# A fused two-layer transformer kernel on one core: where the second attention's negated maxima are copied, and the order of its score products

## What is computed

```python
q = _apply_rotary((x @ wq).reshape(b, s, H, HD), cos, sin)
k = _apply_rotary((x @ wk).reshape(b, s, H, HD), cos, sin)
v = (x @ wv).reshape(b, s, H, HD)
scores = jnp.einsum('bqhd,bkhd->bhqk', q, k) * scale
scores = jnp.where(causal[None, None], scores, jnp.finfo(scores.dtype).min)
probs = jax.nn.softmax(scores, axis=-1)
out = jnp.einsum('bhqk,bkhd->bqhd', probs, v).reshape(b, s, d)
return out @ wo
```

## Time and profile before

| | us |
|---|---|
| median of 3 runs (lowest, highest) | 2004.17 (2003.63, 2010.52) |
| the profiled execution, its own time | 2012.39 |
| its span | 2010.7 |
| first and last copy of maxima (L2018) start at | 1598.4, 1856.3 |
| busy in the span: PE, DVE, ACT, POOL | 1913.5, 1515.4, 914.2, 905.4 |
| mean granted TensorE clock, as a share of full speed | 0.982 |

### The profile page before, as it was taken

The page is one execution under the profiler, slowest core; times in us unless marked ns, Lnnn a source line. Parts: engine busy times, 40 slices in busy tenths (PEclk is TensorE's granted clock), DMA queues, the critical chain, the costliest instruction groups (busy, mean ns, idle before and its releaser), DMA issues.

```text
span 2010.7 us, 41714 instructions
## 1 busy us (share of the span) xinstructions
PE 1913.5 (95%) x14040; PEld 1626.3 (81%) x14040; DVE 1515.4 (75%) x2386; ACT 914.2 (45%) x2297; POOL 905.4 (45%) x872
## 2 busy tenths in 40 slices
PE   8999979999999999999999999988999889998998
PEld 3688869999999999999999999976898755555776
DVE  2576657787777887777888777877888457778886
ACT  1323334444444444444444444445455357777432
POOL 0123354444444444444444444453576557777111
PEclk9999989999999999999999999998999989999999
DMA  9567751111111111111111111411487764443121
GB/s 344 173 209 239 229 161 47 47 47 47 47 47 47 47 44 43 45 43 44 47 47 47 47 47 42 140 35 48 146 252 216 229 193 146 146 142 117 38 63 58
DMA packets 201695, 211.02 MB, mean 105 GB/s; under 512 B 19066, under 2 KB 172666, under 8 KB 200604
## 3 DMA queue, kind: packets, MB, share of 16 engines
q1 hardware_dynamic: 200692, 209.27, 33.6%
q10 hardware_dynamic: 936, 0.85, 0.1%
HBM read 128.14 MB, written 73.53 MB: 100 GB/s over the span
## 4 chain that ended last, share of the span: by engine, by line
PE 68%; issue 13%; DVE 9%; POOL 3%; ACT 3%; SPq 2%; DMA 1%; POOLq 0%; ACTq 0%; DVEq 0%
PE ps L1029 18%; PE ps L990 18%; PE ps L1004 7%; PE ps L1018 4%; PE ps L1041 4%; DVE f_neg_max L1977 3%; PE ps L1013 3%; PE ps L2587 2%; POOL k_rot L565 2%; PE ps L2551 2%; ACT f_q L2018 2%; PE ps L1798 2%; PE ps L2086 2%; PE ps L2092 1%; SPq L1305 1%
## 5 line engine op out<-in xcount | busy, mean ns | idle before, releaser
L1029 PE MATMUL ps<-wo,ot 128*128 (+1 forms) x1536 | 391.0, 404 | 0.1
L1029 PEld LDWEIGHTS ps<-wo,ot 128*128 128x128 f32 x1536 | 283.7, 191 | 61.1 <-issue 1.3
L990 PE MATMUL ps<-ht_hi,wq 128*128 (+1 forms) x2048 | 288.2, 284 | 3.9 <-DVE q_swap L863 3.9
L990 PEld LDWEIGHTS ps<-ht_hi,wq 128*128 128x128 f32 x2048 | 269.0, 192 | 9.7 <-DVE q_swap L863 4.1
L790 ACT ACTIVATE prob<-ps,neg_max 128x128 f32<-128x128 f32 (+1 forms) x512 | 208.3, 421 | 130.1 <-DVE neg_max L870 108.0
L947 POOL TENSOR_TENSOR q_rot<-q_rot,q_swap 128x512 f32<-128x512 f32 x128 | 164.9, 1288 | 201.5 <-DVE q_swap L863 196.9
L797 ACT ACTIVATE pt<-ps 128x512 fp32r<-128x512 f32 x192 | 107.7, 597 | 302.8 <-PE ps L1041 302.8
L942 POOL TENSOR_TENSOR prob<-prob,inv_sum 128x512 f32<-128x512 f32 x64 | 66.6, 1040 | 291.0 <-DVE inv_sum L879 291.0
L1977 DVE TENSOR_REDUCE f_neg_max<-ps 128x4 f32<-128x512 f32 (+1 forms) x128 | 122.3, 957 | 62.4 <-PE ps L2086 60.6
L990 PE MATMUL ps<-ht_lo,wq 128*128 (+1 forms) x1024 | 165.5, 284 | 0.0
L1004 PE MATMUL ps<-pt,vv 128*128 128x512 f32 x576 | 148.7, 402 | 9.3 <-issue 8.6
(11 more groups left out here) (245 smaller groups left out, 4168.5 us busy)
## 6 DMA issues: line engine op xcount, KB each, us to landing
stack_dram<-e_part SPq DMA_DIRECT2D x192, 128.0 KB, 2.4
v_dram<-v_part SPq DMA_DIRECT2D x32, 512.0 KB, 5.7
k_dram<-k_part SPq DMA_DIRECT2D x64, 256.0 KB, 2.7
kk<-k_dram SPq DMA_DIRECT2D x128, 128.0 KB, 2.1
vv<-v_dram SPq DMA_DIRECT2D x128, 128.0 KB, 2.1
f_q<-stack_dram SPq DMA_DIRECT2D x124, 104.0 KB
f_k<-stack_dram SPq DMA_DIRECT2D x124, 104.0 KB
wmod<-in_wmod SPq DMA_DIRECT2D x12, 1024.0 KB, 11.8
```

Source lines behind the costliest of these rows:

```text
L990: mm = nc.tensor.matmul(ps_q[j][:, e], w[:, c:c + HD0], r[:, bass.ds(u % B, 1), k].rearrange("p o s -> p (o s)"), start=(n == 0), stop=(n ...
L1029: mm = nc.tensor.matmul(ps_y[j][:], o[:, j, h * P:(h + 1) * P], w[:, bass.ds(at + h * D, D)], start=(n == 0), stop=(n == len(passes) - 1))
```

## The change

The second copy of the negated maxima no longer reads PSUM: it is issued behind the unit's two exponentials in ScalarE's step, and reads the first copy from SBUF. The late scores wait for the first copy alone. `near` is computed ahead of `far` and of the early scores, and both wait for both exponentials of the unit before; the exponentials and the cuts follow in the order near, far. The exponential that waits for VectorE's first maximum is now the second of the two.

```diff
--- before.py
+++ after.py
@@ -2014,8 +2014,12 @@
 
             act.wait_ge(m_done, u + 1)
             src = max_rows.rearrange("p (o s) -> p o s", o=1).broadcast_to([HU, 2, S])
-            for e in range(2):
-                nc.scalar.activation(q[slot][64 * e:64 * e + HU], src, ACT.Identity).then_inc(m_out, 1)
+            nc.scalar.activation(q[slot][0:HU], src, ACT.Identity).then_inc(m_out, 1)
+
+        def negated_again(u, slot):
+
+            act.wait_ge(m_out, 2 * u + 1)
+            nc.scalar.activation(q[slot][64:64 + HU], f32(q[slot][0:HU]), ACT.Identity).then_inc(m_out, 1)
 
         def high(w):
 
@@ -2026,9 +2030,9 @@
         def exponentials(u, slot, at):
             if at >= 2:
                 act.wait_ge(o_done, u - 1)
-            for j, (p, sc) in enumerate(((prob1, t1), (prob0, t0))):
+            for j, (p, sc) in enumerate(((prob0, t0), (prob1, t1))):
                 act.wait_ge(t_done, 4 * u + 2 * j + 2)
-                if j == 0 and at < U - 2:
+                if j and at < U - 2:
                     act.wait_ge(smax, 2 * u + 5)
                 nc.scalar.activation(p[slot % 2][:].rearrange("p (e i) s -> p e i s", e=2), sc, ACT.Exp,
                                      scale=SCALE1).then_inc(p_exp, 1)
@@ -2038,6 +2042,8 @@
                 negated(v + 1, (slot + 1) % NS)
             if 0 <= at < U:
                 exponentials(v, slot, at)
+            if -1 <= at < U - 1:
+                negated_again(v + 1, (slot + 1) % NS)
             if at in (0, 1):
                 load_unit(act, keep, NS + v, v)
             if 5 <= at and slot % 2:
@@ -2052,7 +2058,7 @@
     def gpsimd(pool):
         def cut(u, slot):
 
-            for j, p in enumerate((prob1[slot % 2][:], prob0[slot % 2][:, :, 0:P])):
+            for j, p in enumerate((prob0[slot % 2][:, :, 0:P], prob1[slot % 2][:])):
                 pool.wait_ge(p_exp, 2 * u + j + 1)
                 nc.gpsimd.nop(nofuse=True)
                 nc.gpsimd.affine_select(p, p, pattern=[[0, HU], [1, P]], compare_op=ALU.is_ge, fill=0.0,
@@ -2095,7 +2101,7 @@
     def scores_late(pe, u, slot, first=False):
 
         if not first:
-            pe.wait_ge(m_out, 2 * u)
+            pe.wait_ge(m_out, 2 * u - 1)
         for e in range(2):
             put_mask(1, e)
         for e in range(2):
@@ -2181,20 +2187,17 @@
             if 0 <= at < U:
                 pe.wait_ge(m_out, 2 * v + 2)
                 if at > 0:
-                    pe.wait_ge(p_exp, 2 * v - 1)
+                    pe.wait_ge(p_exp, 2 * v)
                 if at < U - 2:
                     mask_early()
+                shifted_near(v, slot)
                 shifted_far(v, slot)
             if 0 <= at < U - 2:
                 scores_early(pe, v + 2, (slot + 2) % NS)
-            if 0 <= at < U:
-                if at > 0:
-                    pe.wait_ge(p_exp, 2 * v)
-                shifted_near(v, slot)
             if -1 <= at < U - 2:
                 scores_late(pe, v + 2, (slot + 2) % NS)
             if at == U - 1:
-                pe.wait_ge(p_exp, 2 * U - 1)
+                pe.wait_ge(p_exp, 2 * U)
             if at >= TAIL:
                 side(pe, at - TAIL)
             if 1 <= at:
```

## The result

The change takes 1992.28 us (median of 6 runs, 1989.61 to 1992.67), the kernel before, in runs beside it, 2006.26 (6 runs, 2003.63 to 2010.52). The ratio is 0.9926, 95% interval 0.9913 to 0.9939: 14.8 us less. The forecast was 1990.2 us, 14.0 less than a kernel before of 2004.2. The profiled execution of the change took 1990.09 us, its span is 1988.4.

What follows compares the result with a forecast made beforehand. No engine is full; a loop of waits through TensorE, ScalarE and VectorE sets the 3.84 us step. Middle 11.7 + opening 2.2 + tail 1.0 - end 0.9 = 14.0 us less, from 2004.2 to 1990.2 us; range 1985 to 1999.

Steps and rivals of the forecast that it cites:

- The loop: Middle step of the second attention: the chain of waits from transposes to next transposes falls from 3.84 to 3.58 us.
- TensorE is late next: Middle step: of 0.60 us taken off the loop only 0.26 are gained, as TensorE's own work delays the late mask.
- the middle: The 45 middle steps of the second attention: 0.26 us gained in each, 11.7 us in all; 5.9 with the upper bound.
- granted clock below 1.00 in the middle steps: A sign in the profile of the change that would show the forecast wrong: TensorE below full clock there.
- The other paths: Four paths in a middle step, among them VectorE's reductions and ScalarE's second copy, that must fit into 3.58 us.
- The rivals: Middle, late second copy: wait only moves (step 3.84 at 1.10 us of copy), chance 0.09; slower (from 1.4 us), 0.06.
- The opening: First steps of the second attention, with two waits for loads: 2.2 us gained, bounds 1 and 3.
- The tail: Six steps with pieces of the next stage: 4.05 us each instead of 4.22, 1.0 us gained; bounds 0.5 lost, 2.5 gained.
- The end: Last unit: the next stage's product waits for both exponentials instead of the small one alone, 0.9 us lost.

Runs made afterwards that it cites:

- the edit of the last unit: The change, but in the last unit alone far, its exponential and its cut come first and the next stage's product waits for that exponential only: 1990.47 us, ratio 0.9913.

## Why the prediction was right, and where it was not

**The loop.** The prediction's sum for a step was 3.58 us, measured is 3.54, or 3.53 without the first step. The mechanism is as predicted, and shown from both sides: without the copy's move the late mask stays at 1.66 and the step at 3.84, and the masks' wait for ScalarE, 8.6 us before, is gone in the change. "TensorE is late next" is shown too: taking the early mask out of TensorE's way gave 3.36. The term that was mis-sized is the way from the transposes to the late mask, 1.36 instead of 1.40, and with it the middle, 13.7 instead of 11.7. That TensorE's blocks keep their sum when they are permuted held within 0.04 us here; with `far` behind the late scores it did not hold. The sign "granted clock below 1.00 in the middle steps" came true in the first of the 45 steps alone, as it had before the change.

**The other paths.** VectorE's first reduction was put at 1.57 to 1.68 after the transposes with "up to 0.07" lost; it starts at 1741.94 - 1740.44 = 1.50, and nothing is lost. The late reduction still waits for TensorE, but by 0.07 us a step only. The second copy was put at 0.63 us from a copy of 128 partitions; it takes 0.627. The Trainium skill's page "ScalarE: Activation LUTs" (section What ACT_TABLE_LOAD costs) had given an estimated 0.61; the trace's 0.627 lies 2 to 3% above it.

**The price of a late copy.** The rivals said that the step returns to 3.84 with a copy of 1.10 us. The loop is there, but its constant is 2.5 to 2.6 us, not 2.74, and the point is near 1.35. In the step shown with 1.32 us of copies the chain is the prediction's, and its links tell where the 0.26 went: early mask to first reduction 1.29 (1746.28 to 1747.57) where the sum had 1.36; the exponential of `far` ends at 1748.89, but the first copy starts at 1748.79, 0.10 before, where the sum put it behind; and the three copies take 1.24 from the first start to the last end where they add up to 1.32. So the overlap of one ScalarE instruction with the next was left out, though the prediction had read 0.1 of it in the pair of exponentials. The rivals with this loop had a chance of 0.15 between them; the run with the old order of exponentials shows such a loop deciding, at 4.03 a step.

**The opening.** Predicted 2.2; the two executions of the change give 3.5 and 2.3. From the first transposes to the load that TensorE waits for it is 38.74 us (40.13 before), 1.4 less for the 1.1 predicted, and from there to the next transposes 4.18 (4.71), 0.53 for 0.6. The rest lies behind that load: the next three steps, of which the prediction counted 0.24, take 10.70 us (11.88 before), with 3.63 at a granted clock of 0.97 in the first of them (4.20 at 0.83 before). The two executions of the change differ in the wait for that load (5.35 and 4.29), in the wait for the next one (0.95 and 1.64), and in the fourth step, 4.50 us at 0.76 in one and 5.96 at 0.51 in the other. The size stays open: over all kernels here the opening takes 56.8 to 64.9 us, and which steps run at the lower clock was not tried.

**The tail.** Predicted 4.05 a step, measured 3.94, and the reason given was for the most part wrong. ScalarE was said to hold it, with its first copy late. A step of the change:

```profile
1827.59 1.28 POOL L2070 TENSOR_TENSOR f_both<-f_prob,f_prob 128x512 f32<-128x512 f32 x1
...
1827.96 0.57 ACT L2017 ACTIVATE f_q<-ps 4x512 fp32r<-4x512 f32 x1
...
1828.30 1.12 DVE L2443 TENSOR_TENSOR g_lo<-g_raw,g_w 128x512 fp32r<-128x512 f32 x1
...
1828.61 0.39 PE L2098 MATMUL ps<-mask_b,ident_b 128*128 128x256 bf16 x2
...
1829.34 1.81 DVE L1977 TENSOR_REDUCE f_neg_max<-ps 128x4 f32<-128x512 f32 x2
...
1831.21 0.38 PE L2129 MATMUL ps<-ident,f_neg_max 128*4 128x128 f32 x2 [0.55 <-DVE f_neg_max L1977]
```

The copy ends at 1828.53, ahead of the late mask at 1828.61; in two of the six steps the mask does wait for it, 0.22 us. VectorE holds: g_lo (L2443) ends at 1829.42 and both reductions follow it with no idle time, and the transposes wait for them (0.55). Over the six steps VectorE is busy for 23.42 of 23.63 us, before for 23.25 of 25.34, when it waited for the late scores. The overlap of f_both with g_lo, which the prediction weighed with the Trainium skill's page "GPSIMD Engine Reference" (section Specifications), did not go away: f_both runs from 1827.59 to 1828.87, over g_lo's start. The eight g_lo of the change take 0.97 to 1.14 us, where before 1.35 and 0.69 took turns. That agrees with the page's contention of two-input instructions, and the 2.0 us that would have come back by it did not. It is not overlap as such that makes g_lo long, as the prediction read the earlier trace rows: the short g_lo before (1835.19 to 1835.88) overlaps an f_both too, but one that starts behind it, at 1835.42, and then f_both is the long one, 1.59 us for 1.27. Where f_both started first, g_lo ended 0.54 to 0.55 us behind its end, before (1831.80 and 1832.34) and in the change (1828.87 and 1829.42). In the change f_both starts first in all of the six steps. What came back, 1.7, is the idle time of VectorE, and the order alone brings it, as the run without the copy's move shows (23.67); which part of the order does it was not tried.

**The end.** Predicted 0.9 lost; 0.94 in the profile, and 0.98 given back by the edit of the last unit. The span's end is a further 0.8 us later, which no run explains; it varies by as much between executions (from that product on it is 149.9 us in one execution of the change, 150.4 in the other, and 149.0 before).

**The whole.** 14.0 us predicted, 14.8 by the ratio. (The time itself, 1992.28, is 2.1 above the forecast of 1990.2, since the kernel before took 2006.26 beside it and not 2004.17.) In the profile the terms were 2.0 too small in the middle, 1.3 in the opening and 0.7 in the tail, and the end lost 0.9 more: 17.1 in all. The other execution of the change gives 15.8 by the same stretches. That the timed runs say 14.8 and not 17.1 lies within what two executions differ by, so the sum is no more exact than the 3 us between it and the profile.

## What to carry over

When a wait is taken off a loop, add up what its waiter still has to do itself: of the 0.60 us taken off only 0.31 were gained, because TensorE was late next, and the next gain lay in TensorE's own order. Two halves of a change can each be worthless or harmful and pay together; cost the moved operation in the order that it will stand in, by what its engine waits for there. And an operation with time to spare may stand in either place only until its neighbour has none: the copy between the exponentials cost nothing with the early mask behind the transposes, and 0.18 us a step with it ahead.

## What the runs showed of the hardware

On TensorE the order of blocks has a price of its own: `far` takes 0.28 us ahead of the early block, which has its shape, and 0.37 ahead of the products with 32-column weights of the values. Two masks in fp32r take 0.44 us to the next block, in bf16 0.32; their weight loads are busy for 189 and 97 ns. On ScalarE a further copy of 0.40 us ahead of another lengthened the step by only 0.07, and 0.69 us by 0.27; instructions issued behind one another overlapped by up to 0.10. Of f_both (GpSimd) and g_lo (VectorE) the one that started second became longer: g_lo ended 0.54 to 0.55 us behind f_both however much of it lay under it (1.35 us with 0.81 of overlap, 1.12 with 0.57, 0.89 with 0.34 in the kernel with two added copies), and kept its 0.69 where it started first, while f_both took 1.59 instead of 1.27. And the step behind the last wait for a load ran at a lower granted clock in most executions: 3.92 us at 0.90 in the change (3.54 at 1.00 in the other execution of it), 6.03 at 0.52 with the fp32r masks, where the steps after it take 3.53 and 3.68.
